# Query phase of a gated cross-attention and expert layer: two tiles normalised early, the scale moved into the bias, the spreading of the integers moved to ACT

## What is computed

```
x = x + tanh(g0) * xattn(layernorm(x), ctx)
x = x + tanh(g1) * moe(layernorm(x))

xattn:  q = (x @ Wq + bq) / sqrt(32)      16 heads of 32 numbers
        k, v = ctx @ Wkv + bkv
        q, k: per token and head  s = max(|.|) / 127, at least 1e-8;  round(. / s) * s
        v:    the same along the keys
        attn = softmax(q k^T), rounded to 255 steps;  out = attn v;  out @ Wp + bp
```

## Time and profile before

| what | value |
|---|---|
| median of three runs | 1052.98 us |
| the profiled execution's own time | 1052.83 us |
| its span, first to last instruction | 1051.3 us |
| mean granted clock of PE in it | 0.982 of full speed |
| PE busy in the span | 981.4 us, 93% |
| DVE busy | 638.5 us, 61% |
| ACT busy | 496.0 us, 47% |
| POOL busy | 445.8 us, 42% |

### The profile page before, as it was taken

The page is one execution under the profiler, slowest core; times in us unless marked ns, Lnnn a source line. Parts: engine busy times, 40 slices in busy tenths (PEclk is TensorE's granted clock), DMA queues, the critical chain, the costliest instruction groups (busy, mean ns, idle before and its releaser), DMA issues.

```text
span 1051.3 us, 16610 instructions
## 1 busy us (share of the span) xinstructions
PE 981.4 (93%) x5718; PEld 497.3 (47%) x5719; DVE 638.5 (61%) x1141; ACT 496.0 (47%) x1051; POOL 445.8 (42%) x311
## 2 busy tenths in 40 slices
PE   5899999879999999999999899999999999999994
PEld 2334444324434444444444456555655665566551
DVE  4896766589999999999999755811111111111156
ACT  2023222259999999999999922111221122112210
POOL 1043333317887777677776830271111111111165
PEclk9999999989999999999999998999999999999997
DMA  8955646669888878888887644154544655643155
GB/s 312 233 188 206 211 182 206 204 145 146 144 135 132 128 139 141 138 146 143 128 144 110 101 180 171 55 193 138 182 176 179 232 185 199 234 163 142 50 162 160
DMA packets 268272, 172.45 MB, mean 164 GB/s; under 512 B 239344, under 2 KB 239344, under 8 KB 265904
## 3 DMA queue, kind: packets, MB, share of 16 engines
q1 hardware_dynamic: 258512, 140.14, 54.9%
q0 software_dynamic: 9696, 31.47, 8.8%
HBM read 68.67 MB, written 44.63 MB: 108 GB/s over the span
## 4 chain that ended last, share of the span: by engine, by line
PE 52%; POOL 18%; DVE 13%; issue 8%; ACT 5%; DMA 3%; SPq 0%; POOLq 0%; DVEq 0%; ACTq 0%
PE ps L746 18%; POOL arena_a L1447 14%; PE ps L766 9%; PE ps L581 6%; PE ps L598 5%; PE ps L558 5%; ACT arena_a L914 4%; DVE span_max L1128 3%; POOL expert_in L1465 2%; PE ps L683 2%; PE ps L640 2%; PE ps L776 1%; PE ps L757 1%; DVE proj_i L1072 1%; DVE amax L1066 1%
## 5 line engine op out<-in xcount | busy, mean ns | idle before, releaser
L1128 DVE TENSOR_REDUCE span_max<-ps 128x1 f32<-128x481 f32 (+2 forms) x400 | 351.4, 904 | 19.8 <-PE ps L598 11.7
L914 ACT ACTIVATE arena_a<-ps,exp_bias,q_step 128x962 uint8<-128x962 f32 (+1 forms) x288 | 329.9, 1157 | 23.3 <-DVE exp_bias L1148 12.5
L1447 POOL CAST arena_a<-arena_a 128x3072 bf16<-128x3072 uint8 x100 | 273.9, 2746 | 122.3 <-DMA arena_a<-arena_a 115.5
L598 PE MATMUL ps<-arena_a,q_t 128*128 128x481 bf16 (+1 forms) x864 | 225.4, 374 | 19.5 <-DVE span_max L1128 7.1
L746 PE MATMUL ps<-arena_a,xt 128*128 x544 | 172.2, 459 | 1.7 <-issue 1.7
L1284 DVE TENSOR_TENSOR proj_d<-ps,proj_f 128x352 f32<-128x352 f32 x48 | 25.2, 524 | 200.0 <-ACT proj_f L962 200.0
L968 ACT COPY proj_r<-ps 128x128 f32<-128x128 f32 x144 | 28.4, 270 | 224.2 <-PE ps L757 224.2
L766 PE MATMUL ps<-arena_a,proj_r 128*128 (+3 forms) x288 | 133.5, 600 | 0.7 <-ACT proj_r L968 0.7
L598 PEld LDWEIGHTS ps<-arena_a,q_t 128*128 128x128 bf16 x864 | 62.3, 98 | 150.2 <-ACT arena_a L914 71.0
L746 PEld LDWEIGHTS ps<-arena_a,xt 128*128 128x128 f32 x544 | 100.4, 190 | 61.2 <-issue 17.8
L581 PE MATMUL ps<-arena_a 128*128 128x512 f32 (+1 forms) x192 | 83.0, 578 | 6.3 <-ACT xt L877 4.0
(11 more groups left out here) (166 smaller groups left out, 933.1 us busy)
## 6 DMA issues: line engine op xcount, KB each, us to landing
arena_a<-in_w_up SPq DMA_DIRECT2D x18, 1408.0 KB, 6.4
arena_a<-in_w_down SPq DMA_DIRECT2D x18, 768.0 KB, 8.4
key_parts<-parts SPq DMA_DIRECT2D x23, 512.0 KB, 2.7
expert_in<-xt SPq DMA_DIRECT2D x42, 256.0 KB, 3.0
xt<-expert_in POOLq DMA_DIRECT2D x36, 256.0 KB, 3.0
expert_out<-xt POOLq DMA_DIRECT2D x34, 256.0 KB, 2.3
arena_a<-in_ctx_t SPq DMA_DIRECT2D x3, 1536.0 KB, 13.8
expert_out<-xt SPq DMA_DIRECT2D x17, 256.0 KB, 3.1
```

The lines of the kernel that those rows point to most:

```text
L598: last = mm(ps[:, bank + b, 0:w], q_t[:, head, t * P:(t + 1) * P], k_t[head % NK][:, a:a + w], start=True, stop=True)
L914: nc.scalar.activation(halves[:, :, a:a + w], ps[:, bank:bank + 2, 0:w], ACT.Exp, bias=exp_bias[:, n % 2:n % 2 + 1], scale=step_of, accum_ ...
L1128: v.tensor_reduce(span_max[:, n % 2, j:j + 1], ps[:, bank:bank + len(blocks), 0:w], AX.XY, ALU.max).then_inc(s_max, 1)
L1447: p.tensor_copy(p_t[n % NPT].rearrange("p c q -> p (c q)").rearrange("p (j i) -> p j i", j=2), pt_u8[n % NT8].rearrange("p (i j) -> p j i" ...
```

## The change

- The first two tiles (`FIRST` = 2) are normalised right after their own statistics; tile t - 1 is normalised after those of tile t only from t = 3 on. ACT takes the first two roots, copies the first two transposed tiles, and goes on as before from the third.
- POOL multiplies the query row of the bias by `QSCALE` in place, once, after all seven small loads (`s_qbias`). The read-out of a query product is then one instruction, product times `QSCALE` plus bias, and the multiplication at line 1065 is gone.
- The read-outs of the first two query projections move into the layer norm of DVE, behind tiles 4 and 6; the wait for the small loads and for `s_qbias` moves there too, to tile 4.
- The spread moves from DVE to ACT (`spread_query`); DVE signals the integers with `s_qint`. The integers of j = 2 to 8 wait for the spread of j - 2. ACT does the spread of tile 0 before it copies the last transposed tile, and the spreads of tiles 1 to 6 after it; from tile 2 on each waits for the transpose two before.
- The negated steps are made by POOL, one small instruction per query tile; DVE waits for all of them before attention.
- The second layer norm has the same order of work as before, written with the new functions.

```diff
--- before.py
+++ after.py
@@ -269,6 +269,9 @@
         s_mid = sem("middle_part_ready")
         s_parts = sem("low_part_ready")
         s_fourth = sem("fourth_part_zeroed")
+        s_qbias = sem("query_bias_scaled")
+        s_qint = sem("query_integers_made")
+        s_nq = sem("negative_query_steps_ready")
         s_qi = sem("query_integers_ready")
         s_qt = [sem("query_transposed_0"), sem("query_transposed_1")]
         s_kp = [sem("key_parts_stored_0"), sem("key_parts_stored_1")]
@@ -344,6 +347,8 @@
 
 
         LEAD = 3
+
+        FIRST = 2
         NP = T + KT
 
         def spread(a, shape):
@@ -389,7 +394,7 @@
                 if t == T - 1:
                     sp.wait_ge(s_pad, 1)
                 sp.dma_start(x_sb[0:rows, t, :], x[t * P:t * P + rows, :]).then_inc(s_x[t], 16)
-                if t == 1:
+                if t == FIRST - 1:
                     sp.dma_start(w_qkv[:, 0, :, :], wq.rearrange("(k p) n -> p k n", p=P)).then_inc(s_wq, 16)
             sp.dma_start(bias_rows[:, 0, :], bq.unsqueeze(0).to_broadcast([P, D])).then_inc(s_small, 16)
             sp.dma_start(bias_rows[:, 1, :], bkv[0:D].unsqueeze(0).to_broadcast([P, D])).then_inc(s_small, 16)
@@ -862,11 +867,28 @@
                 act.wait_ge(s_var, (n - 1) * T + t + 1)
                 nc.scalar.activation(std[:, t:t + 1], std[:, t:t + 1], ACT.Sqrt).then_inc(s_std, 1)
 
-            for t in range(T + 1):
+            def spread_query(j):
+
+                act.wait_ge(s_qint, j + 1)
+                if j >= 2:
+                    act.wait_ge(s_qt[j % 2], 16 * (j // 2))
+                nc.scalar.copy(parts[:, j % 2].rearrange("p h g d -> p g h d"),
+                               proj_i[:, j % 2, :].rearrange("p (h d) -> p h d", h=H).unsqueeze(1)
+                               .to_broadcast([P, HG, H, HD])).then_inc(s_qi, 1)
+
+            for t in range(FIRST):
+                root(1, t)
+            for t in range(FIRST):
+                copy_transposed(t, s_tr, 0, s_xt, x_t)
+            root(1, FIRST)
+            for t in range(FIRST + 1, T + 1):
                 if t < T:
                     root(1, t)
-                if t:
-                    copy_transposed(t - 1, s_tr, 0, s_xt, x_t)
+                copy_transposed(t - 1, s_tr, 0, s_xt, x_t)
+                if t >= T - 1:
+                    spread_query(t - (T - 1))
+            for j in range(2, T):
+                spread_query(j)
             def copy_values(v):
 
                 g, c = divmod(v, NV)
@@ -1007,21 +1029,43 @@
                 ins.then_inc(s_dve, 1)
                 dve.wait_ge(s_dve, chain[0])
 
-            def layer_norm(n, prepare):
-
-                for t in range(T + 1):
-                    if t < T:
-                        prepare(t)
-                        link(v.bn_stats(stats[:, t, :], x_sb[:, t, :]))
-                        link(v.bn_aggr(mean_var[:, t, :], stats[:, t, :]))
-                        v.tensor_scalar_add(std[:, t:t + 1], mean_var[:, t, 1:2], LN_EPS).then_inc(s_var, 1)
-                    if t:
-                        dve.wait_ge(s_std, (n - 1) * T + t)
-                        link(v.reciprocal(std[:, t - 1:t], std[:, t - 1:t]))
-                        v.tensor_scalar(xn[:, t - 1, :], x_sb[:, t - 1, :], mean_var[:, t - 1, 0:1],
-                                        std[:, t - 1:t], ALU.subtract, ALU.mult).then_inc(s_xn, 1)
-
-            layer_norm(1, lambda t: dve.wait_ge(s_x[t], 16))
+            def moments(n, t):
+
+                link(v.bn_stats(stats[:, t, :], x_sb[:, t, :]))
+                link(v.bn_aggr(mean_var[:, t, :], stats[:, t, :]))
+                v.tensor_scalar_add(std[:, t:t + 1], mean_var[:, t, 1:2], LN_EPS).then_inc(s_var, 1)
+
+            def normed(n, t):
+
+                dve.wait_ge(s_std, (n - 1) * T + t + 1)
+                link(v.reciprocal(std[:, t:t + 1], std[:, t:t + 1]))
+                v.tensor_scalar(xn[:, t, :], x_sb[:, t, :], mean_var[:, t, 0:1],
+                                std[:, t:t + 1], ALU.subtract, ALU.mult).then_inc(s_xn, 1)
+
+            def read_projection(j):
+
+                pf = proj_f[:, j % 2, :]
+                dve.wait_ge(s_proj, j + 1)
+                if j < T:
+                    v.scalar_tensor_tensor(pf, ps[:, 2 + j % 2, :], QSCALE, bias_rows[:, 0, :],
+                                           ALU.mult, ALU.add).then_inc(s_pf, 1)
+                else:
+                    v.tensor_tensor(pf, ps[:, 2 + j % 2, :], bias_rows[:, 1, :], ALU.add).then_inc(s_pf, 1)
+
+
+            for t in range(T):
+                dve.wait_ge(s_x[t], 16)
+                moments(1, t)
+                if t < FIRST:
+                    normed(1, t)
+                elif t > FIRST:
+                    normed(1, t - 1)
+                if t == 4:
+                    dve.wait_ge(s_small, 16 * 7)
+                    dve.wait_ge(s_qbias, 1)
+                if t in (4, 6):
+                    read_projection(t // 2 - 2)
+            normed(1, T - 1)
 
             def bound_values(v_):
 
@@ -1049,34 +1093,26 @@
                 v.tensor_copy(v_b.rearrange("p (j i) -> p j i", j=2)[:, :, 0:PAIRS], v_i[:, :, 0:PAIRS]).then_inc(s_vb, 1)
 
 
-            dve.wait_ge(s_small, 16 * 7)
             for j in range(NP):
                 b = j % 2
                 kt = j - T
                 pf = proj_f[:, b, :]
                 heads = lambda a: a.rearrange("p (h d) -> p h d", h=H)
-                dve.wait_ge(s_proj, j + 1)
-                chain[0] += 1
-                ins = v.tensor_tensor(pf, ps[:, 2 + b, :], bias_rows[:, 0 if j < T else 1, :], ALU.add)
-                ins.then_inc(s_pf, 1)
-                chain[0] -= 1
+                if j >= 2:
+                    read_projection(j)
                 dve.wait_ge(s_pf, j + 1)
-                if j < T:
-                    link(v.tensor_scalar(pf, pf, QSCALE, None, ALU.mult))
                 link(v.tensor_reduce(amax[:, b, :], heads(pf), AX.X, ALU.max, apply_absolute_value=True))
                 st = q_step[:, :, j] if j < T else step[:, b, :]
                 link(v.tensor_scalar(st, amax[:, b, :], 1.0 / 127.0, 1e-8, ALU.mult, ALU.max))
+                link(v.reciprocal(inv_step[:, b, :], st))
+                if 2 <= j < T + 2:
+                    dve.wait_ge(s_qi, j - 1)
+                integers = v.tensor_tensor(heads(proj_i[:, b, :]), heads(pf), spread(inv_step[:, b, :], [P, H, HD]),
+                                           ALU.mult)
                 if j < T:
-                    v.tensor_scalar(neg_q_step[:, :, j], st, -1.0, None, ALU.mult)
-                link(v.reciprocal(inv_step[:, b, :], st))
-                link(v.tensor_tensor(heads(proj_i[:, b, :]), heads(pf), spread(inv_step[:, b, :], [P, H, HD]), ALU.mult))
-                if j < T:
-                    if j >= 2:
-                        dve.wait_ge(s_qt[b], 16 * (j // 2))
-                    v.tensor_copy(parts[:, b].rearrange("p h g d -> p g h d"),
-                                  proj_i[:, b, :].rearrange("p (h d) -> p h d", h=H).unsqueeze(1)
-                                  .to_broadcast([P, HG, H, HD])).then_inc(s_qi, 1)
+                    integers.then_inc(s_qint, 1)
                 else:
+                    link(integers)
                     if kt >= 2:
                         dve.wait_ge(s_rest, kt - 1)
                         dve.wait_ge(s_hi, kt - 1)
@@ -1103,6 +1139,8 @@
             dve.wait_ge(s_buf, NP8 + 1)
             dve.wait_ge(s_tail, 16 * HG)
             link(v.tensor_scalar(neg_tail_step[:, :], tail_step[:, :], -1.0, None, ALU.mult))
+
+            dve.wait_ge(s_nq, T)
 
             def invert(inv, sums):
 
@@ -1171,7 +1209,12 @@
                                        ALU.mult, ALU.add).then_inc(s_x1, 1)
                 dve.wait_ge(s_x1, t + 1)
 
-            layer_norm(2, residual)
+            for t in range(T + 1):
+                if t < T:
+                    residual(t)
+                    moments(2, t)
+                if t:
+                    normed(2, t - 1)
 
 
 
@@ -1408,6 +1451,11 @@
             pool.wait_ge(s_zero, 3)
             p.tensor_scalar(thresholds[:, :], tile_no[:, 1:T], float(P), None, ALU.mult).then_inc(s_pool, 1)
 
+            pool.wait_ge(s_small, 16 * 7)
+            p.tensor_scalar(bias_rows[:, 0, :], bias_rows[:, 0, :], QSCALE, None, ALU.mult).then_inc(s_qbias, 1)
+            for j in range(T):
+                pool.wait_ge(s_qint, j + 1)
+                p.tensor_scalar(neg_q_step[:, :, j], q_step[:, :, j], -1.0, None, ALU.mult).then_inc(s_nq, 1)
             pool.wait_ge(s_proj, T)
             p.memset(zero_tile, 0.0).then_inc(s_ztile, 1)
```

## The result

Seven runs of the changed kernel gave 1044.37 to 1049.44 us, with a median of 1047.07. Seven runs of the kernel before, beside them, gave 1052.01 to 1056.87, with a median of 1052.64. The ratio is 0.9936, with a 95% interval of 0.9917 to 0.9955: faster by 0.64%, which is 6.7 us (4.7 to 8.7). This ratio is an estimate from the runs and not the quotient of the two medians, which lie 5.6 us apart, inside that interval. The median is 2.5 above the forecast of 1044.6 and inside its range.

What follows compares the result with a forecast made beforehand. DVE was taken to bound the kernel from 38.2 to 78.3, before PE carries it. Key tile 2 starting 8.2 earlier, all else kept, gave 1052.83 - 8.2 = 1044.6 us; range 1042.3 to 1049.0.

Steps and rivals of the forecast that it cites:

- The start: Query phase start: first projection at 10.1, DVE's wait for the scaled bias ends at 17.9, third projection at 23.9, 1.9 earlier.
- The clock: PE's gap before the third projection, 19.8 to 23.9: a low clock had cost 1.9 elsewhere; nothing was charged.
- the rule that was set against the forecast: Waits between matmul bursts throttle PE again, so the third projection would run slowly; the sum about 0.5 longer.
- The spread: Query tiles, spread on ACT: 1.9 to 2.0 us each, upper end 2.45, lower end 0.69.
- Rival 4: Query tiles: ACT is slow at the spread; break-even at 4.7 us each, at 7 the kernel takes 1059.8; chance 0.04.
- The first landing: First query transpose: lands at 38.2 as before, its time set by the loads it stands behind.
- Rival 2: First query transpose: not tied to the loads, lands 1.8 earlier, PE sets the pace; 9.7 won, 1043.1; chance 0.09.
- The round trip of a transpose: Query tiles 2, 4, 6: a transpose lands 4.5 after its spread; three spreads and two transposes end at 53.2.
- What takes DVE's place: Key tiles: ACT, POOL and stores give the first value block's copy at about 69.3, under DVE; third value block 70.1.
- rival 1: Key tiles: the key pipeline hangs on the last transpose; third value block at 73.1, 5.2 won, 1047.6; chance 0.16.
- What follows: Roots, the statistics loop of the second layer norm and everything after: unchanged, counted as nothing.
- Rival 3: After the query phase: the gain is given back by PE's low clock or unchanged attention start; 1048 to 1053; chance 0.11.

Runs made afterwards that it cites:

- vals: Changed kernel, with ACT copying value blocks 18 and 19 before the first copy of the last key tile: median 1046.48 us, ratio 0.9929 to the kernel before.
- loads: Changed kernel, with the last context piece and the value weights issued after the seven query transposes: median 1046.04 us, ratio 0.9917 to the kernel before.
- bias alone: Changed kernel, with the query bias on its own semaphore, so POOL scales it without awaiting the other six small loads: median 1047.85 us, ratio 0.993.
- own room: Changed kernel, with each query tile spread into its own buffer space, so no spread waits for a transpose: median 1043.16 us, ratio 0.9883.

## Why the prediction was right, and where it was off

**The start** held. First projection 10.1 predicted, 10.20 measured; scaling on POOL 1.56, 1.51; end of DVE's wait 17.9, 17.80; third projection 23.9, 24.15. The first projection's eight matmuls took 6.34, where 3.60 is their time later, with the clock shown at 1.00 in the stretches from 10.2 to 16.2. That was not foreseen and its cause is open, but DVE waited for the bias beside it. That two tiles normalised early would not keep their gain is borne out by the run with one.

**The clock** stayed at 1.00 at the third projection in the profile of the changed kernel, as charged. That was luck: in its repetition, and in two of the eleven variants, it fell to 0.50 just there, and the third projection took 1.0 to 1.7 longer. So the rule that was set against the forecast, of the Trainium skill, page "TensorE: Matmul & The Clock Gate", section "HAM oscillation — how this bites in real kernels", bit in 3 of 13 profiles, and in these three it did not help that transposed tiles broke the gap. Charging nothing for the value block came out right all the same: in the repetition and in `vals` the block stood 33.45 behind the first landing, as in the executions without the fall.

**The spread** held: 1.95 predicted, 1.897 measured, with 3.70 for two in a row. The Trainium skill, page "ScalarE: Activation LUTs", section "What ACT_TABLE_LOAD costs", gives 186 ns and 0.833 ns per element for an instruction without pointer operands; for 2048 that is an estimate of 1.89, and the trace agrees. Rival 4 (ACT slow at 16-bit integers) is out.

**The first landing** held: 38.2 predicted, 38.34 measured. Rival 2, that it is not tied to the loads, is refuted twice: issued anywhere from 24.8 to 28.9, it landed at 37.2 to 39.8; with two loads behind it, it landed about 5.0 after its issue at 26.53. The last load of the changed kernel shows what it is tied to:

```profile
L411 SPq DMA_DIRECT2D arena_a<-in_wkv x1: 3745/3745/3745, 18.7 to 18.7; - x1
...
DMA to landing us min/median/max: 17.0/17.0/17.0
```

That load landed at 35.7 and the transpose 2.6 behind it. In the 13 profiles with all loads ahead the first transpose landed 1.8 to 3.4 behind the last of them, and in `loads` 1.9 behind the last that was still ahead.

**The round trip of a transpose was mis-sized.** "Tile 2 is spread at 38.25 to 40.2 and its transpose lands 4.5 later at 44.7": it landed 6.25 later, at 46.60. All six executions that still have two halves, ACT's spread and the first transpose behind the loads (the changed kernel twice, one early tile, scale on DVE, bias alone, value copies alone) show 6.24 to 6.26 there, and 5.84 to 5.88 for tile 3 behind it. The 4.5 was about the median of the rows before, where two of the seven took 5.2 and 5.3; the 5.3 that the forecast kept as a bound was passed as well. Everything behind moved by about as much: tile 6 spread at 53.05 instead of 51.25, key tile 2 read out at 56.38 instead of 54.5, the value block at 71.79 instead of 70.1. The first key copy came at 55.45 instead of 54, the second at 59.28 instead of 57.6. With 6.5 in place of 8.2 the sum would have been 1052.83 - 6.5 = 1046.3; the runs give 6.7 us by the ratio and 5.6 by the medians. Why just these transposes are slow is open: with the last loads behind the transposes no landing exceeds 5.0.

**What takes DVE's place** was judged by a thin margin. The text said that the key relay of ACT, POOL and the stores "hides under DVE", 69.3 against 70.1. The chain shows that relay as the one that ended last, and PE waited 0.89 for ACT's copy at its end; this is the mechanism of rival 1. Its price was not: rival 1 put the value block at 73.1, and the distance from key tile 2 to the value block, 71.79 - 56.38 = 15.4, is near the 15.58 that the forecast kept. That agreement is luck, since another path now sets it. DVE was done with the tile that the copy belongs to at 68.23 + 1.53 = 69.76, and ACT's part of it began only at 70.44, when a store had landed:

```profile
68.23 1.53 DVE L1119 TENSOR_TENSOR proj_d<-proj_i,step 128x512 f32<-128x512 int16 x1
```

So the relay lies 0.7 behind DVE's path, where the forecast had it 0.8 ahead.

**What follows** was taken as unchanged. On the whole it is: from the value block to attention 136.5 before, 136.2 and 134.5 in two profiles of the changed kernel, the last with the shorter value matmuls named above. Single executions differ by some 3 us further on, so the profile shows 4.2 of the 6.5 at the end of the span, and that of the repetition 7.1. Rival 3 (the gain is given back) is not borne out by the ratio.

## What to carry to other kernels

When an engine comes off the path, count the round trips through the buffers it shared: here two halves and three landings took its place, and room for each tile removed them. Where a transfer stands behind loads, its landing goes with the loads and not with its issue. Measure later events from that landing (here 33.4 to 33.5 in six executions); then an effect of the edit is told from a shift of the loads. At the value block an earlier start was worth nothing while that landing held the rest, and 2.0 with own room; in the whole time those 2.0 were not seen. So try such edits together with the cure, not alone. And look at the granted clock in more than one execution before calling a gap harmless.

## What was not expected of the hardware

**The same wait, another clock.** Before its last 32 value matmuls PE idles 3.41 to 3.43 in each kernel without the early value copies. These 32 matmuls then took 12.77 in the repetition of the changed kernel and in the run with one early tile, 14.16 with the last loads behind the transposes, 14.47 in six profiles, and 15.76 and 15.79 in those of the bias alone and of own room alone. PE in order of time and the stretch just behind the wait, first own room, then the repetition (columns as in the earlier trace rows):

```profile
189.25 15.79 PE L594 MATMUL ps<-arena_a 128*128 128x512 f32 x32 [3.42 <-ACT xt L906]
```

```profile
191.00:193.00 2.00, 2.00 (x4) 0.85 (x3) 0.69 (x1) 0.15 (x1) 0.86 (x1) 0.50 0.79 182
```

```profile
192.27 12.77 PE L586 MATMUL ps<-arena_a 128*128 128x512 f32 x32 [3.41 <-ACT xt L899]
```

```profile
193.00:195.00 2.00, 2.00 (x6) 0.81 (x5) 0.69 (x1) 1.17 (x2) 1.16 (x1) 1.00 1.16 216
```

After a wait of the same length the clock stood at 0.50 (1.2 GHz) in one execution and at 1.00 (2.4 GHz) in the other, which costs 0 to 3.0 us. The changed kernel itself shows 14.47 in one profile and 12.77 in the next, and at the third projection 1.00 in one and 0.50 in the other. One profile of each kernel is too few to tell an edit's part in that from chance.

**The scatter.** Runs of the changed kernel differ by 5 us (1044.37 to 1049.44). The clock behind that wait explains up to 3.0 of it. `vals` scatters by 4.3 without the wait, but with another one and the low clock behind that. In the profiles attention takes 387.3 to 390.1 and the stage from there to the experts 39.5 to 42.1. Every run has its mean granted clock, and the time goes with it: the two longest of the seven runs of the changed kernel (1049.18 and 1049.44) are those with the lowest clock, 0.978, and the shortest has 0.983. Over the 25 runs of the kernel before in the first batch the correlation is -0.80, some 0.9 us for each 0.001. That the two go together does not show which is the cause. Beyond the places named here, in which stages the clock differs stays open.
